# Two heads of a cross-attention in the two row halves of TensorE, scores in two matmuls each, values weighed every second slot

## The chip, the core and the metric

The kernel runs on one NeuronCore of a Trainium2 chip. TensorE (PE in the profile, its weight loads PEld) multiplies, VectorE (DVE) finds maxima, ScalarE (ACT) takes exponentials and copies, GpSimd (POOL) splits numbers, and the queue of SyncE (SP) issues DMAs. The metric is device microseconds of one execution: lower is better.

## The reference

The program computes two Perceiver layers: six blocks, each added to x (4 batches, 256 rows, 256 columns). Only the first block is touched by this change. It attends with 16 heads of 16 numbers from the 256 rows of x to a context of 4096 rows of 128 numbers:

```python
qh = (q @ Wq + bq).reshape(B, LQ, HEADS, D_K).transpose(0, 2, 1, 3)     # 4, 16, 256, 16
kh = (k @ Wk + bk).reshape(B, LKV, HEADS, D_K).transpose(0, 2, 1, 3)    # 4, 16, 4096, 16
vh = (v @ Wv + bv).reshape(B, LKV, HEADS, D_K).transpose(0, 2, 1, 3)
scores = jnp.einsum('bhqd,bhkd->bhqk', qh, kh) * scale
attn = jax.nn.softmax(scores, axis=-1)
out = jnp.einsum('bhqk,bhkd->bhqd', attn, vh)
x = x + out.transpose(0, 2, 1, 3).reshape(B, LQ, D_MODEL) @ Wo + bo
```

## The kernel before

`ContextAttention0` does this block. Queries and keys are float32, but their products are taken in bfloat16: each number is split into three bfloat16 parts, and of the nine products of parts the six largest are summed. They are summed by the contraction: `keysT` and `queriesT` hold six parts of 16 rows each under one another (`ROWS` = 96), and two more rows add the negative maximum of each query (its "shift", `AUG` = 98). Values and probabilities stay float32.

A *group* is two heads (`GH`) of one batch, 32 groups in all; four groups are a *unit*, eight a batch. A group has 16 *slots*; a slot is two tiles of 128 keys, 512 slots in all. TensorE's program is one loop over slots t, from -60 (the preparation) to 514. In a slot it does, in this order: scores of the first key tile of both heads (two matmuls of 256 columns, line 540), one matmul of 512 columns for the maxima of a group that lies `LEAD` = 19 slots ahead (line 524), scores of the second key tile, in every fourth slot the weighing of the last four slots (line 559), the second matmul for maxima, and then what the table `due` of `plan()` has for this slot:

- "fill keys" (line 587): 512 keys of a later unit, one float32 matmul, every 8 slots
- "make values" (line 626): two key tiles of the next batch's values, 16 times in a batch
- "turn ctx" (line 578): four transposes, 8 times in a batch
- "turn shift" (line 614) and "normalize" (line 645): once in a group

In three of the four batches this table is the same; the last has no next batch to prepare and has parts of the second block ("stream") instead. Each engine runs the same loop with its own part of each job, in its own program's order, and waits on semaphores.

PSUM has eight banks. Scores go through banks 0, 1 and 2 in turn (`HALVES`), the sums of the weighing through bank 3, and everything else, the maxima too, through 4, 5, 6 and 7 in turn (`misc`). A bank is written again once the engine that reads it has signalled: ACT after the exponential (line 783), DVE after the reduction of a matmul of maxima (line 685).

The weighing has 17 output partitions to a matmul, so four of them stand side by side in the 32-column strips of the array (`k.bank(SUMS)[32 * quad:...]`). All float32 matmuls appear in the trace as two records each.

Keys reach `keysT` through device memory: the parts are written by "write parts" and read back with three DMAs to a group, of 48, 32 and 16 rows to a head (`RUNS`). A group's maxima and scores wait until all of its DMAs have landed.

## Time and profile before

| | |
|---|---|
| median of 3 runs | 1429.02 us (1427.55 to 1429.71) |
| span of the profiled execution | 1429.1 us |
| TensorE's mean granted clock | 0.989 of full |
| first scores start, last weighing ends | 67.1 us, 968 us |
| PE busy | 1375.6 us, 96% |
| DVE, ACT, POOL busy | 74%, 65%, 20% |

The busy time of matmuls is modelled, and matmuls that follow each other overlap in it; what a matmul costs is read here as the distance from its start to the next start. The profiled execution shows its span alone, which lies within 0.1 us of the median.

### The profile page before, as it was taken

How to read it: one execution, taken by the hardware profiler on the slowest of the kernel's cores; microseconds unless marked ns; L12 is line 12 of the kernel's file. 1: busy time of each engine (PE TensorE's matmuls, PEld its weight loads, DVE VectorE, ACT ScalarE, POOL GpSimd, SP SyncE). 2: the span in 40 equal slices, each digit the busy share in tenths (PEclk: the TensorE clock that was granted, in tenths of full speed). 3: DMA queues.
4: the chain of work that ended last, by engine and by line, in shares of the span. 5: the costliest groups of instructions: out<-in, count | busy, mean ns of one | idle time of the engine just before them, and what ended most of it. 6: DMA issues, size and time to landing. Idle time of an engine off the chain costs nothing.

```text
span 1429.1 us, 28070 instructions
## 1 busy us (share of the span) xinstructions
PE 1375.6 (96%) x11138; PEld 846.7 (59%) x11138; DVE 1055.1 (74%) x2114; ACT 922.1 (65%) x1899; POOL 287.6 (20%) x321
## 2 busy tenths in 40 slices
PE   7799999999999999999999999999999999989998
PEld 5355555555555545555554556556557999856666
DVE  4787777787777778777778888835876778767757
ACT  5366777767777767777767666672796664448731
POOL 3354222222222222122213100000003100001210
PEclk9899999999999999999999999999999999999999
DMA  6966555346554545655454743002402320347000
GB/s 184 163 145 143 119 118 111 77 102 130 116 127 92 102 84 125 128 115 113 81 97 101 184 73 61 2 1 60 119 18 65 112 67 1 91 112 155 2 1 30
DMA packets 95587, 133.19 MB, mean 93 GB/s; under 512 B 8864, under 2 KB 70944, under 8 KB 89504
## 3 DMA queue, kind: packets, MB, share of 16 engines
q1 hardware_dynamic: 95456, 131.40, 42.3%
q8 instruction: 88, 1.44, 0.5%
q14 instruction: 43, 0.35, 0.1%
HBM read 94.15 MB, written 37.22 MB: 92 GB/s over the span
## 4 chain that ended last, share of the span: by engine, by line
PE 79%; ACT 8%; DVE 8%; DMA 2%; issue 2%; SPq 1%; POOL 0%; DVEq 0%; ACTq 0%
PE psum L559 16%; PE psum L540 13%; PE psum L524 13%; ACT probs L783 4%; PE psum L2132 4%; PE psum L587 3%; PE psum L2106 3%; DVE peaks L685 3%; PE psum L626 3%; PE psum L1226 2%; PE psum L2851 2%; PE psum L1623 1%; PE psum L275 1%; PE psum L2861 1%; PE psum L2814 1%
## 5 line engine op out<-in xcount | busy, mean ns | idle before, releaser
L685 DVE TENSOR_REDUCE peaks<-psum 128x1 f32<-128x512 f32 x1024 | 643.3, 684 | 197.0 <-PE psum L524 196.4
L783 ACT ACTIVATE probs<-psum 128x512 f32<-128x512 f32 x1024 | 529.0, 615 | 83.3 <-PE psum L540 79.4
L524 PE MATMUL psum<-keysT,queriesT 96*128 96x512 bf16 x1024 | 390.1, 384 | 13.2 <-DMA keysT<-key_parts 7.9
L540 PE MATMUL psum<-queriesT,keysT 98*128 98x256 bf16 x2048 | 392.4, 274 | 6.1 <-ACT queriesT L846 2.4
L540 PEld LDWEIGHTS psum<-queriesT,keysT 98*128 98x128 bf16 x2048 | 176.3, 99 | 191.7 <-ACT probs L783 72.1
L559 PE MATMUL psum<-probs,values 128*17 128x256 f32 x4096 | 245.9, 380 | 0.0
L559 PEld LDWEIGHTS psum<-probs,values 128*17 128x17 f32 x4096 | 107.2, 97 | 102.6 <-issue 27.1
L524 PEld LDWEIGHTS psum<-keysT,queriesT 96*128 96x128 bf16 x1024 | 98.6, 96 | 90.9 <-issue 56.1
L918 POOL CAST key_parts<-key_f 128x512 bf16<-128x512 f32 x57 | 34.8, 611 | 518.0 <-ACT key_f L816 511.0
L816 ACT ACTIVATE key_f<-psum,bk 128x512 f32<-128x512 f32 x59 | 40.5, 687 | 120.7 <-PE psum L587 120.6
L587 PE MATMUL psum<-ctxT,wk 128*128 128x512 f32 x128 | 69.5, 625 | 2.4 <-DVE probs L728 0.9
L924 POOL TENSOR_TENSOR key_parts<-key_r,key_parts 128x512 bf16<-128x512 f32 x57 | 66.0, 1158 | 4.5
L920 POOL TENSOR_TENSOR key_r<-key_f,key_parts 128x512 f32<-128x512 f32 x57 | 65.9, 1157 | 4.5
L2132 PEld LDWEIGHTS psum<-ctx_nat,ring 128*128 128x128 f32 x512 | 64.6, 191 | 3.6 <-ACT ring L2267 0.7
L2132 PE MATMUL psum<-ctx_nat,ring 128*128 128x129 f32 x512 | 65.9, 275 | 0.7 <-ACT ring L2267 0.6
L626 PE MATMUL psum<-wv,ctxT 128*128 128x256 f32 x256 | 65.4, 381 | 0.5 <-DVE probs L716 0.4
L1919 ACT ACTIVATE weights<-psum,peaks 128x256 f32<-128x256 f32 x128 | 58.7, 487 | 10.5 <-DVE peaks L1788 10.3
L2106 PE MATMUL psum<-early_weights,ctx_T 128*128 128x256 f32 x256 | 63.2, 380 | 0.0
L857 ACT ACTIVATE values<-psum 128x512 f32<-128x512 f32 x64 | 38.0, 599 | 29.3 <-PE psum L626 28.5
L2257 ACT ACTIVATE ring<-psum 128x512 f32<-128x512 f32 x64 | 37.7, 596 | 29.1 <-PE psum L2106 28.8
L626 PEld LDWEIGHTS psum<-wv,ctxT 128*128 128x128 f32 x256 | 47.9, 190 | 14.0 <-issue 5.5
L2267 ACT ACTIVATE ring<-ring 128x1024 f32<-128x1024 f32 (+1 forms) x36 | 34.6, 962 | 24.3 <-DVE ring L2177 24.1
(315 smaller groups left out, 1662.5 us busy)
## 6 DMA issues: line engine op xcount, KB each, us to landing
keysT<-key_parts SPq DMA_DIRECT2D x31, 768.0 KB, 7.7
key_parts<-key_parts SPq DMA_DIRECT2D x90, 256.0 KB
keysT<-key_parts SPq DMA_DIRECT2D x31, 512.0 KB, 10.1
ctx_nat<-in_ctx_dram SPq DMA_DIRECT2D x32, 256.0 KB, 3.0
keysT<-key_parts SPq DMA_DIRECT2D x31, 256.0 KB, 11.6
ctx_in<-in_ctx_dram SPq DMA_DIRECT2D x24, 256.0 KB, 5.9
ctx_turned<-ctxT SPq DMA_DIRECT2D x24, 256.0 KB, 4.4
ctx_T<-ctx_turned SPq DMA_DIRECT2D x12, 512.0 KB, 3.8
```

The lines of the kernel that those rows point to most:

```text
L524: e.matmul(ps, self.queriesT[0:ROWS, u % 2, g * GH + j, t * P:(t + 1) * P], self.keysT[0:ROWS, i % RING, j, c * BANK:(c + 1) * BANK], star ...
L540: made = e.matmul(ps[:, j * S:(j + 1) * S], self.keysT[0:AUG, i % RING, j, kt * P:(kt + 1) * P], self.queriesT[0:AUG, u % 2, g * GH + j, : ...
L559: made = e.matmul(k.bank(SUMS)[32 * quad:32 * quad + DH + 1, 0:S], self.values[b % 2][:, kt, g * GH + j, :], self.probs[:, (SLOTS * i + p) ...
L587: e.matmul(ps, self.wk[:, 0, m * P:(m + 1) * P], self.ctxT[:, c * BANK:(c + 1) * BANK], start=True, stop=True).then_inc(*self.key_made.up( ...
L626: made = e.matmul(ps[:, e2 * D:(e2 + 1) * D], self.ctxT[:, kt * P:(kt + 1) * P], self.wv[:, 0, :], start=True, stop=True)
L685: e.tensor_reduce(self.peaks[:, i % 2, pair, c:c + 1], k.ps(("max", n)), AX.X, ALU.max).then_inc(*self.peaked.up(n))
L783: e.activation(self.probs[:, t % RINGP, e2 * GH * S:(e2 + 1) * GH * S], k.ps(("scores", t, e2)), ACT.Exp).then_inc(*self.exped.up((t, e2)))
L920: e.tensor_tensor(self.key_r[:, :], k_f, part(0), ALU.subtract).then_inc(*w.up(self.split_pool, ("rest",) + key))
L924: e.tensor_tensor(part(2), self.key_r[:, :], part(1), ALU.subtract).then_inc(*w.up(self.split_pool, ("part2",) + key))
L1919: made = e.activation(self.weights[:, (2 * q + i) % self.NR, kt, :], k.ps(("scores3", q, i))[:, kt * S:(kt + 1) * S], ACT.Exp, bias=self.p ...
L2106: made = e.matmul(ps[:, i * S:(i + 1) * S], l.ctx_T[:, b % 2, kt * P:(kt + 1) * P], l.qcT[:, b * S:(b + 1) * S], start=True, stop=True)
L2132: made = e.matmul(k.ps(("weigh4", b, i))[:, 0:C + 1], self.at(n)[:, column:column + P], l.ctx_nat(b % 2)[:, kt, :], start=(kt == 0), stop= ...
```

## The change

A head's six products no longer stand in 98 rows. Each head has one half of the 128 rows: head 0 rows 0 to 63, head 1 rows 64 to 127. `keysT` and `queriesT` have two planes: MAIN holds four products (64 rows), REST the other two and the shift (34 rows). The scores of a key tile are now two matmuls to a head, MAIN and REST, summed in PSUM; the four matmuls of the two heads alternate between the halves. The maxima are taken over MAIN alone (four of the six products; the shift needs no more), and the matmuls of maxima of the two heads follow each other directly. A bank of scores now holds both key tiles of one head, and there are four such banks (0, 1, 2, 4); three are left for the rest (5, 6, 7). The weighing is done every second slot, in the odd ones, for two slots. Values, keys and transposes of the context are moved to even slots. Reads of keys are six DMAs of 32 rows instead of three; parts 0 and 1 of the queries are written twice.

```diff
 GH = 2
 PARTS = 3
 RUNS = ((0, 3), (3, 2), (5, 1))
-PAIRS = 6
-ROWS = PAIRS * DH
-AUG = ROWS + 2
+KEY_AT = (1, 2, 0)
+QUERY_AT = ((2, 3), (0, 1), (4,))
+HALF = P // 2
+MAIN, REST = 0, 1
+LOW = 2 * DH
+TALL = LOW + 2
 NG = H // GH
 GROUPS = B * NG
 SLOTS = LC // P // 2
@@ -308,7 +311,7 @@
 TOTAL = GROUPS * SLOTS
 FIRST = -60
 RINGP = 6
-HALVES, SUMS = 3, 3
+SCORES, SUMS, BLOCK = (0, 1, 2, 4), 3, 2
...
-        self.keysT = sb(scope, "keysT", [P, RING, GH, LC], BF16)
+        self.keysT = sb(scope, "keysT", [P, 2, RING, LC], BF16)
         self.values = [values, sb(scope, "values1", [P, LC // P, H, DH + 1])]
-        self.queriesT = sb(scope, "queriesT", [P, 2, P // DH, S], BF16)
+        self.queriesT = sb(scope, "queriesT", [P, 2, 2, UNIT_GROUPS, S], BF16)
...
-                slot = UNIT * u - 101 + 8 * c
+                slot = UNIT * u - 100 + 8 * c
...
-                at(SLOTS * NG * b - 97 + 6 * p, "make values", b, p)
+                at(SLOTS * NG * b - 96 + 8 * (p // 2) + 2 * (p % 2), "make values", b, p)
...
-            choice = (7, 0, 1, 2) if t < -1 else (4, 5, 6, 7)
+            choice = (7, 0, 1, 2) if t < -1 else (5, 6, 7)
...
-            e.matmul(ps, self.queriesT[0:ROWS, u % 2, g * GH + j, t * P:(t + 1) * P],
-                     self.keysT[0:ROWS, i % RING, j, c * BANK:(c + 1) * BANK],
-                     start=True, stop=True).then_inc(*self.max_made.up(n))
+            e.matmul(ps, self.queriesT[own, MAIN, u % 2, g, qt * P:(qt + 1) * P],
+                     self.keysT[own, MAIN, i % RING, c * BANK:(c + 1) * BANK],
+                     start=True, stop=True).then_inc(*self.max_made[j].up(n))
...
-            for e2 in range(2):
-                if 0 <= t < TOTAL:
-                    kt, n = 2 * p + e2, (2 * t + e2) % HALVES
-                    ps = banks.use(n, w, ("scores", t, e2), (self.exped, (t, e2)))
-                    for j in range(GH):
-                        made = e.matmul(ps[:, j * S:(j + 1) * S], self.keysT[0:AUG, i % RING, j, kt * P:(kt + 1) * P],
-                                        self.queriesT[0:AUG, u % 2, g * GH + j, :], start=True, stop=True)
-                    made.then_inc(*self.scored.up((t, e2)))
-                if maxima and not e2:
-                    find_max(maxima[0], t)
-            if t % 4 == 1 and 5 <= t <= TOTAL + 1:
-                i, p0 = divmod(t - 5, SLOTS)
+                ps = {}
+                for e2 in range(2):
+                    kt = 2 * p + e2
+                    for plane, rows in ((MAIN, HALF), (REST, TALL)):
+                        for j in range(GH):
+                            if j not in ps:
+                                ps[j] = banks.use(SCORES[(2 * t + j) % len(SCORES)], w, ("scores", t, j), (self.exped, (t, j)))
+                            own = slice(j * HALF, j * HALF + rows)
+                            made = e.matmul(ps[j][:, e2 * S:(e2 + 1) * S], self.keysT[own, plane, i % RING, kt * P:(kt + 1) * P],
+                                            self.queriesT[own, plane, u % 2, g, :], start=(plane == MAIN), stop=(plane == REST))
+                            if e2 and plane == REST:
+                                made.then_inc(*self.scored[j].up((t, j)))
+            for n in maxima:
+                find_max(n, t)
+            if t % BLOCK == 1 and BLOCK + 1 <= t <= TOTAL + 1:
+                i, p0 = divmod(t - BLOCK - 1, SLOTS)
                 b, g = divmod(i, NG)
                 w.wait_ge(self.exped, (t - 2, 1))
-                for p in range(p0, p0 + 4):
+                for p in range(p0, p0 + BLOCK):
                     w.wait_ge(self.v_kept, (b, p))
                 w.wait_ge(self.ones_set, b % 2)
                 if i:
                     w.wait_ge(self.outT_kept, i - 1)
                 w.wait_ge(self.cleared, 0)
-                for p in range(p0, p0 + 4):
+                for p in range(p0, p0 + BLOCK):
                     for e2 in range(2):
                         for j in range(GH):
-                            quad, kt = e2 * GH + j, 2 * p + e2
+                            quad, half, kt = e2 * GH + j, 2 * j + e2, 2 * p + e2
                             made = e.matmul(k.bank(SUMS)[32 * quad:32 * quad + DH + 1, 0:S],
                                             self.values[b % 2][:, kt, g * GH + j, :],
-                                            self.probs[:, (SLOTS * i + p) % RINGP, quad * S:(quad + 1) * S],
+                                            self.probs[:, (SLOTS * i + p) % RINGP, half * S:(half + 1) * S],
                                             start=(p == 0), stop=(p == SLOTS - 1))
-                made.then_inc(*self.weighed.up((t - 5) // 4))
-            for n in maxima[1:]:
-                find_max(n, t)
+                made.then_inc(*self.weighed.up((t - BLOCK - 1) // BLOCK))
...
-        return divmod(r, CH) if i else divmod(r, GH * QT)[::-1]
+        step, j = divmod(r, GH)
+        qt, c = divmod(step, CH) if i else divmod(step, QT)[::-1]
+        return i, j, qt, c
...
-                for e2 in range(2):
-                    w.wait_ge(self.scored, (t, e2))
-                    e.activation(self.probs[:, t % RINGP, e2 * GH * S:(e2 + 1) * GH * S], k.ps(("scores", t, e2)),
-                                 ACT.Exp).then_inc(*self.exped.up((t, e2)))
+                for j in range(GH):
+                    w.wait_ge(self.scored[j], (t, j))
+                    e.activation(self.probs[:, t % RINGP, 2 * j * S:(2 * j + 2) * S], k.ps(("scores", t, j)),
+                                 ACT.Exp).then_inc(*self.exped.up((t, j)))
...
-                    e.activation(self.queriesT[ROWS:AUG, u % 2, g * GH:(g + 1) * GH, :].rearrange("p h n -> p (h n)"),
-                                 k.ps(("shiftT", i)).bitcast(BF16)[ROWS:AUG, 0:GH * S], ACT.Copy).then_inc(
-                        *self.shiftT_kept.up(i))
+                    for j in range(GH):
+                        own = slice(j * HALF + LOW, j * HALF + TALL)
+                        e.activation(self.queriesT[own, REST, u % 2, g, :], k.ps(("shiftT", i)).bitcast(BF16)[own, 0:S],
+                                     ACT.Copy).then_inc(*self.shiftT_kept.up(i if j else ("first", i)))
...
-                        e.dma_start(self.q_dram[b, :, n, :, :, :].rearrange("h d m n -> h d (m n)"),
-                                    self.q_parts[:, n, :]).then_inc(*self.q_out.up(b))
+                        for copy in QUERY_AT[n]:
+                            e.dma_start(self.q_dram[b, :, copy, :, :, :].rearrange("h d m n -> h d (m n)"),
+                                        self.q_parts[:, n, :]).then_inc(*self.q_out.up(b))
...
-                    for block, run in RUNS:
-                        e.dma_start(self.queriesT[block * DH:(block + run) * DH, u % 2, :, :],
-                                    self.q_dram[b, :, 0:run, :, m, :].rearrange("h i d n -> (i d) h n")).then_inc(
-                            *self.rows_here[u % 2].up(u))
+                        for j in range(GH):
+                            w.wait_ge(self.scored[j], (UNIT * (u - 1) - 1, j))
+                    for plane, rows, parts in ((MAIN, HALF, slice(0, 4)), (REST, LOW, slice(3, 5))):
+                        for j in range(GH):
+                            e.dma_start(self.queriesT[j * HALF:j * HALF + rows, plane, u % 2, :, :],
...
-        for block, run in RUNS:
-            e.dma_start(self.keysT[block * DH:(block + run) * DH, i % RING, :, keys],
-                        self.key_dram[u, g * GH:(g + 1) * GH, PARTS - run:PARTS, :, keys].rearrange(
-                            "j i d n -> (i d) j n")).then_inc(*landed.up(key))
+        for j in range(GH):
+            for row, plane, first in ((0, MAIN, 1), (LOW, MAIN, 1), (0, REST, 0)):
+                e.dma_start(self.keysT[j * HALF + row:j * HALF + row + LOW, plane, i % RING, keys],
+                            self.key_dram[u, g * GH + j, first:first + 2, :, keys].rearrange("i d n -> (i d) n")).then_inc(
+                    *landed.up(key))
```

In the order of instructions on PE the change looks as follows in the middle of a unit (x counts matmuls as written). Names: `psum<-queriesT,keysT` are scores, `psum<-keysT,queriesT` maxima, `psum<-probs,values` the weighing, `ctxT,wk` the keys of a later unit. Before:

```order
L540 MATMUL psum<-queriesT,keysT 128x256 x2
L559 MATMUL psum<-probs,values 17x256 x16
L524 MATMUL psum<-keysT,queriesT 128x512
L587 MATMUL psum<-ctxT,wk 128x512
L540 MATMUL psum<-queriesT,keysT 128x256 x2
L524 MATMUL psum<-keysT,queriesT 128x512
L540 MATMUL psum<-queriesT,keysT 128x256 x2
L524 MATMUL psum<-keysT,queriesT 128x512
```

The same engine after the change, in the second half of a batch, from an odd slot over an empty even slot to one with keys and shift (lines are numbered anew: 546 scores, 527 maxima, 566 weighing, 592 keys, 620 shift):

```order
L566 MATMUL psum<-probs,values 17x256 x8
L546 MATMUL psum<-queriesT,keysT 128x256 x8
L527 MATMUL psum<-keysT,queriesT 128x512 x2
L546 MATMUL psum<-queriesT,keysT 128x256 x8
L527 MATMUL psum<-keysT,queriesT 128x512 x2
L566 MATMUL psum<-probs,values 17x256 x8
L546 MATMUL psum<-queriesT,keysT 128x256 x8
L527 MATMUL psum<-keysT,queriesT 128x512 x2
L592 MATMUL psum<-ctxT,wk 128x512
L620 MATMUL psum<-ident_b,shift_b 2x128 x4
```

What moved: the matmuls of maxima stand in pairs, the weighing comes in halves twice as often, and preparation never stands directly behind a weighing. Counted over the 512 slots, the array passes between full (128x128), column strips (128x32) and row halves (64x128) 882 times after and 316 times before.

The second place is the queue of SP in the preparation, from the first keys to the second write of keys. Before:

```order
L971 DMA key_parts<-key_parts 8x16x1024 x3
L996 DMA q_parts<-q_parts 8x16x512 x3
L1019 DMA keysT<-key_parts 48x2x1024
L1019 DMA keysT<-key_parts 32x2x1024
L1019 DMA keysT<-key_parts 16x2x1024
L1005 DMA queriesT<-q_parts 48x8x256
L1005 DMA queriesT<-q_parts 32x8x256
L1005 DMA queriesT<-q_parts 16x8x256
L971 DMA key_parts<-key_parts 8x16x1024 x3
```

After:

```order
L980 DMA key_parts<-key_parts 8x16x1024 x3
L1008 DMA q_parts<-q_parts 8x16x512 x5
L1034 DMA keysT<-key_parts 32x1024 x6
L1019 DMA queriesT<-q_parts 64x4x256 x2
L1019 DMA queriesT<-q_parts 32x4x256 x2
L980 DMA key_parts<-key_parts 8x16x1024 x3
```

Six more DMAs stand ahead of the second write of keys, in a queue that issues them one after another.

## Rows read from the trace of the kernel before

**Rows 1.** The page: span, and costliest groups (busy us, mean ns | idle before).

```profile
span 1429.1 us, 28070 instructions
...
L685 DVE TENSOR_REDUCE peaks<-psum 128x1 f32<-128x512 f32 x1024 | 643.3, 684 | 197.0 <-PE psum L524 196.4
...
L540 PEld LDWEIGHTS psum<-queriesT,keysT 98*128 98x128 bf16 x2048 | 176.3, 99 | 191.7 <-ACT probs L783 72.1
```

**Rows 2.** Stretches of 128 slots: length, then busy us of PE, PEld, DVE, ACT, POOL.

```profile
317.00:538.00 221.00, 219.39 (x1988) 118.50 (x1984) 167.52 (x306) 159.91 (x313) 56.60 (x64) 1.00 0.55 110
538.00:759.00 221.00, 219.40 (x1988) 118.53 (x1984) 167.51 (x306) 159.90 (x313) 56.61 (x64) 1.00 0.54 109
```

**Rows 3.** PE's timeline around a weighing (start us, modelled length, line).

```profile
502.39 0.38 PE L540 MATMUL psum<-queriesT,keysT 98*128 98x256 bf16 x2
502.61 0.38 PE L524 MATMUL psum<-keysT,queriesT 96*128 96x512 bf16 x1
502.83 0.38 PE L540 MATMUL psum<-queriesT,keysT 98*128 98x256 bf16 x2
...
505.33 0.39 PE L540 MATMUL psum<-queriesT,keysT 98*128 98x256 bf16 x2
505.65 1.92 PE L559 MATMUL psum<-probs,values 128*17 128x256 f32 x32
507.50 0.39 PE L524 MATMUL psum<-keysT,queriesT 96*128 96x512 bf16 x1
507.73 1.03 PE L626 MATMUL psum<-wv,ctxT 128*128 128x256 f32 x4
508.60 0.38 PE L540 MATMUL psum<-queriesT,keysT 98*128 98x256 bf16 x2
```

**Rows 4.** PE's timeline at a transpose of the context and at a shift.

```profile
340.68 0.60 PE L578 MATMUL psum<-const,ctx_in 128*128 128x128 f32 x4
341.12 0.38 PE L540 MATMUL psum<-queriesT,keysT 98*128 98x256 bf16 x2
...
541.40 0.38 PE L524 MATMUL psum<-keysT,queriesT 96*128 96x512 bf16 x1
541.71 0.38 PE L614 MATMUL psum<-ident_b,shift_b 128*2 128x128 bf16 x4
542.02 0.39 PE L540 MATMUL psum<-queriesT,keysT 98*128 98x256 bf16 x2
```

**Rows 5.** Waits: us in total, times, longest.

```profile
PEld psum L540 <- ACT probs L783: 72.1, 245, 0.8
```

**Rows 6.** PE's timeline in the third block: row strips (L1623), column strips (L1642).

```profile
1046.77 1.13 PE L1623 MATMUL psum<-qT,kT 32*128 32x256 f32 x8
1047.83 1.07 PE L1642 MATMUL psum<-weights,v_scaled 128*32 128x256 f32 x16
1048.83 1.16 PE L1623 MATMUL psum<-qT,kT 32*128 32x256 f32 x16
1049.92 0.42 PE L1642 MATMUL psum<-weights,v_scaled 128*32 128x256 f32 x4
```

**Rows 7.** Timelines of a matmul of maxima and of the reductions behind it.

```profile
46.75 1.38 DVE L685 TENSOR_REDUCE peaks<-psum 128x1 f32<-128x512 f32 x2
...
48.18 0.39 PE L524 MATMUL psum<-keysT,queriesT 96*128 96x512 bf16 x1 [0.31 <-DVE peaks L685]
...
500.86 0.39 PE L524 MATMUL psum<-keysT,queriesT 96*128 96x512 bf16 x1
...
501.29 0.69 DVE L685 TENSOR_REDUCE peaks<-psum 128x1 f32<-128x512 f32 x1 [1.34 <-PE psum L524]
502.59 4.28 DVE L685 TENSOR_REDUCE peaks<-psum 128x1 f32<-128x512 f32 x7 [0.61 <-PE psum L524]
```

**Rows 8.** The preparation: SP's timeline, and the chain that ended last.

```profile
18.04 2.71 SPq L996 DMA_DIRECT2D q_parts<-q_parts  x3
...
46.74 15.22 DMA keysT<-key_parts
```

More of the change, by code:

```diff
@@ L431, in plan @@
                 if c % 2:
-                    at(slot + 7, "write parts", u, c // 2)
+                    at(slot + 6, "write parts", u, c // 2)
         for u in range(B * KD):
@@ L978, in sync @@
                     n, first, last = CONST_COLS["ones"]
-                    for r in range(ROWS, AUG):
-                        e.dma_start(self.keysT[r:r + 1, :, :, :].rearrange("o r h n -> o (r h n)").bitcast(F32).rearrange(
-                            "o (p n) -> o p n", p=P), io["const"][:, first:last].unsqueeze(0)).then_inc(*self.ones_in.up(0))
+                    for r in (LOW, LOW + 1, HALF + LOW, HALF + LOW + 1):
+                        e.dma_start(self.keysT[r:r + 1, REST, :, :].rearrange("o r n -> o (r n)").bitcast(F32).rearrange(
+                            "o (p n) -> o p n", p=P), io["const"][:, first:(first + last) // 2].unsqueeze(0)).then_inc(
+                            *self.ones_in.up(0))
                 elif job == "load x":
```

39 lines of the change are left out of this document (21 added, 18 removed).

## The prediction

> **What bounds the kernel now.** I read the page first. One matmul of maxima is reduced in 684 ns on DVE, 1024 of them, and DVE has idle time in front of them that ends with TensorE; of TensorE's weight loads 72.1 us wait for the exponentials [rows 1, 5]. So ACT and DVE wait for PE most of the time, and PE for them some of it. The windows say how much: 128 slots, one batch, take 221.0 us, and PE is busy for 219.4 of them [rows 2]. A busy PE proves little, so I rebuilt the batch from start-to-start distances. Two score matmuls take 0.22 us and a matmul of maxima takes 0.22 [rows 3], so a slot is four such steps, 0.88. A weighing of 32 records takes 1.85 from 505.65 to 507.50. The two score matmuls ahead of it took 0.32 instead of 0.22, so going into column strips costs 0.10; a record of 256 float32 columns takes 0.87 / 4 = 0.217 alone, eight rounds of four side by side 1.73, so coming out costs 0.12 [rows 3]. Values take 0.87 [rows 3] and keys, two records of twice the columns, I count alike; a transpose of the context takes 0.44, a shift 0.31 + 0.09 [rows 4]; a gather of the heads I count like the shift, 0.40.
>
> A batch: 128 x 0.88 = 112.6, 32 weighings x 1.95 = 62.4, 32 keys and values x 0.87 = 27.8, 8 contexts x 0.44 = 3.5, 16 shifts and gathers x 0.40 = 6.4; together 212.7. Measured are 221.0, so PE itself is the bound, and 8.3 us of a batch are waits, most of them for the exponentials that hold the three score banks [rows 5].
>
> **The change part by part.** *Maxima.* Two matmuls of different row tiles can run side by side. The third block shows it: 8 records of 32 rows, two heads alternating, take 1.06 us (1046.77 to 1047.83), and 16 records of four heads take 1.09 [rows 6]. So a pair of maxima costs one matmul and a few ns, 0.23 instead of 0.44: 128 x -0.21 = -26.9 us a batch.
>
> *Scores.* Eight matmuls instead of four, in four rounds of two: 4 x 0.11 = 0.44 a slot, as before. Nothing is gained here; the same columns are streamed twice, by two heads at once. The bound from above is in the rivals.
>
> *Passages between tilings.* 0.10 in and 0.12 out [rows 3]; from column strips to row strips and back 1.00 - 0.87 = 0.13 and 1.06 - 0.87 = 0.19 with float32 weights that load longer [rows 6]. In a batch of the new order I count 224 passages against 79 (64 weighings and 44 even slots with a job, two each, and 8 between keys and shift). I take 0.105, near the bfloat16 rows: 145 x 0.105 = +15.2 us. The ends are 0.09 (+13) and 0.14 (+20). Nothing hides them, since they lie on PE. The Trainium skill (TensorEngine Tiling (Array Packing), section Tiling Modes) says that changing the tiling mode drains the array; the trace agrees, with 0.10 to 0.12 at each end of a weighing. By its speedup table alone, without that rule, the sum would keep the whole of the -26.9.
>
> *Three banks for maxima and jobs.* Both maxima of a slot are now issued together and need two of three banks. A reduction starts 0.43 after its matmul (500.86 to 501.29), the next 0.60 later ((4.28 - 0.68) / 6), each is 0.68 long, and PE starts 0.05 after its end (48.13 to 48.18) [rows 7]. So the first bank of a pair is free 1.16, the second 1.76 after the pair's start. How far away the next need is depends on the slot:
> - Even slot without a job (20 a batch, and some 90 in all): the next pair starts 0.23 + 0.44 = 0.67 later, and its second matmul needs the first bank: 1.16 - 0.68 = 0.48 of waiting; 9.6 us.
> - Context alone (4 a batch): the next pair is 0.67 + 0.44 + 0.22 = 1.33 away, and needs both banks: 0.43; with a gather as well (4) the gather itself waits some 0.4. Gather alone (4): 0.5. Together 5.3 us.
> - Keys and values (32): 0.67 + 0.87 + 0.22 = 1.76 away, just enough: 0.02, 0.6 us.
> Together +15.5 us a batch. From below it is 0, if PE would have stood still there anyway; the odd slots leave it no such excuse, as DVE has 2.4 us of work in the 2.4 us of PE of an empty even and an odd slot.
>
> *Waits that go.* Four score banks hold two whole slots, and ACT has 160 us of work in 221 [rows 2]; a weighing lasts 0.87 instead of 1.73. I expect almost all of the 8.3 to go and leave 1: -7.3. What is late next is the second matmul of maxima in odd slots.
>
> *Keys, values, contexts moved to even slots:* the same work, 0. They are what keeps the even slots from being empty. *Two small copies of the shift instead of one* lie on ACT, a slot and a half ahead of their use: 0.
>
> *Preparation.* SP issues the writes of queries at 2.71 / 3 = 0.90 each [rows 8]; two more are 1.8, five more reads in that stretch some 0.45 each, 2; SP stood waiting for landings for part of it. What ends the preparation is a read of keys that takes 15.2 us [rows 8] and moves the same bytes as before. I take +3, between 0 and +6.
>
> **The sum.** A batch: -26.9 + 15.2 + 15.5 - 7.3 = -3.5. The last batch has no keys and values, more empty slots and as few passages; I count it alike. 4 x -3.5 = -14, for gaps between my rows and a real batch (keys with a shift, three normalizations of x) +3, preparation +3: -8. The span 1429.1 becomes 1421; span and median lie within 0.1 us, so the median too.
>
> **The rivals.** *Slower by dear passages.* If each passage costs 0.14 as between strips in the third block, the 566 more that the order shows cost 79 instead of 59, and 1421 becomes 1441. The place is the exit of each weighing and each job in an even slot; the sum changes sign at 0.12. For it: the exit at 507.50 already shows 0.12, and the first two weight loads of a row pair come unprepared. Against it: the extra in the third block is with float32 weights.
>
> *Much slower: the weights of the two halves are loaded one after another.* A slot has eight loads of scores, 99 ns each [rows 1], 0.79 instead of 0.44: +0.35 x 512 = +179 less the waits that vanish in it, about 1580. Against it: 16 loads to 1.09 us in the third block [rows 6], 68 ns each and of float32. This is also the case in which the change does not do what it says. The Trainium skill (TensorE: Matmul & The Clock Gate, section LDWEIGHTS) says that a load's time goes by its columns and not by its rows, so 34 rows load no faster than 128; the page's 128 / 1.2, an estimate of 107 ns, would give 0.85 a slot and some 1600.
>
> *Faster: full array to row halves is cheap.* If only the column strips of the weighing cost a passage, 312 passages x 0.105 = -33, about 1388. For it: no bfloat16 row shows this passage. Against it: a shift, bfloat16 in column strips, shows 0.09 on entering [rows 4].
>
> *Faster by less waiting.* If the 0.48 of the even slots were mostly there before as other waits, up to -25: 1396.
>
> **How the numbers follow.** Forecast (PE bound, passages near 0.105, bank waits as worked out, 1400 to 1436): 0.58. Dear passages or more waits, 1433 to 1450: 0.24. Serial weights: 0.06. Cheap passages or fewer waits, 1385 to 1400: 0.12. A measurement of this kernel can tell 0.2%, 2.9 us. Of the forecast two thirds lie under 1426, a sixth within 0.2%; with the other cases faster 0.53, same 0.12, slower 0.35. The range leaves out the serial weights and the ends of the other cases: 1390 to 1447.
>
> **What would show it.** Matmuls of maxima in pairs under 10 ns apart, and then 0.22 to the next start: the gain. Two score matmuls starting together and 0.11 to the next two. In odd slots behind an empty even one, the second matmul of maxima starts about 0.48 after the first, with DVE's reduction as releaser. PE's steps around each weighing and each job 0.09 to 0.12 longer than the columns. Loads of scores waiting for exponentials nearly gone. A batch of 217 to 218 us instead of 221.0, and first scores near 70 us. I am wrong if the two halves don't overlap, if DVE (167.5 us of work in a batch) makes PE wait in most slots and not in the few that I counted, or if keys land late, which would show as long waits of the first maxima of a group for DMAs.

## The result, and the profile after

Measured side by side, the changed kernel takes 1445.26 us (median of 4 runs, 1441.35 to 1447.82) and the kernel before 1429.37 (1427.55 to 1430.82): a ratio of 1.0091, 95% interval 1.0065 to 1.0117 (the two medians alone give 1.011). It became 0.9% slower where 0.6% faster was forecast. The profiled execution is the fastest of the four. In the runs on record the time is about 1.8 us longer than the span of the same execution, and so the span before, 1429.1 us, fits the slowest of its four runs, 1430.82, and not the median. The profiled span after is 1439.6 us, 10.5 more than before; the accounts below are made against that span.

The page of the changed kernel, its costliest groups (busy us, mean ns | idle before, and what ended it):

```profile
L693 DVE TENSOR_REDUCE peaks<-psum 128x1 f32<-128x512 f32 x1024 | 650.2, 685 | 192.4 <-PE psum L527 191.3
...
L546 PEld LDWEIGHTS psum<-queriesT,keysT 64*128 64x128 bf16 (+1 forms) x4096 | 168.5, 95 | 176.0 <-ACT probs L791 121.3
...
L527 PEld LDWEIGHTS psum<-keysT,queriesT 64*128 64x128 bf16 x1024 | 68.6, 94 | 99.7 <-DVE peaks L693 83.6
```

The last row is the new one: the weight loads of the maxima (line 527) now wait 83.6 us for reductions. The row of scores names 121.3 us of waits for exponentials, more than before [rows 5]. That alone says little: a loader that has nothing to do while the array is still busy is idle too. What counts is the distance from start to start on PE.

The windows, one for each batch, from its first scores to those of the next, for the last batch to those of its last slot (length, then busy us of PE, PEld, DVE, ACT, POOL). After:

```profile
66.70:298.90 232.20, 226.09 (x2517) 111.95 (x2517) 175.41 (x322) 172.61 (x330) 74.95 (x86) 0.99 0.47 119
298.90:520.80 221.90, 217.31 (x2500) 105.89 (x2496) 170.17 (x306) 168.20 (x322) 56.53 (x65) 1.00 0.45 110
520.80:742.70 221.90, 217.31 (x2500) 105.92 (x2496) 170.17 (x306) 168.09 (x322) 56.54 (x65) 1.00 0.45 109
742.70:975.40 232.70, 219.96 (x2518) 116.88 (x2516) 174.06 (x353) 154.24 (x299) 25.53 (x28) 1.00 0.29 72
```

And before, the first and the last batch (the middle ones are in [rows 2]):

```profile
67.10:296.70 229.60, 225.24 (x1988) 124.32 (x1987) 173.22 (x322) 163.82 (x321) 75.36 (x86) 1.00 0.55 117
738.70:962.80 224.10, 217.65 (x2021) 127.22 (x2022) 172.55 (x354) 150.82 (x292) 25.29 (x28) 1.00 0.37 74
```

So the batches changed by +2.6, +0.9, +0.9 and +8.6 us, where the forecast had -3.5 for each. The preparation is 0.4 us shorter (66.7 against 67.1) and what follows the last weighing 1.5 shorter.

PE's timeline of the changed kernel in a middle batch (start us, modelled length, line) has nearly every kind of slot that holds a job:

```profile
430.34 0.62 PE L546 MATMUL psum<-queriesT,keysT 64*128 64x256 bf16 x8
430.80 0.38 PE L527 MATMUL psum<-keysT,queriesT 64*128 64x512 bf16 x2
431.11 1.06 PE L566 MATMUL psum<-probs,values 128*17 128x256 f32 x16
432.10 0.62 PE L546 MATMUL psum<-queriesT,keysT 64*128 64x256 bf16 x8
...
432.86 0.66 PE L583 MATMUL psum<-const,ctx_in 128*128 128x128 f32 x4
433.45 0.62 PE L546 MATMUL psum<-queriesT,keysT 64*128 64x256 bf16 x8
433.91 0.79 PE L527 MATMUL psum<-keysT,queriesT 64*128 64x512 bf16 x2
434.63 1.06 PE L566 MATMUL psum<-probs,values 128*17 128x256 f32 x16
...
436.07 0.38 PE L527 MATMUL psum<-keysT,queriesT 64*128 64x512 bf16 x2
436.38 1.13 PE L592 MATMUL psum<-ctxT,wk 128*128 128x512 f32 x2
437.44 0.28 PE L620 MATMUL psum<-ident_b,shift_b 128*2 128x128 bf16 x4
437.65 0.62 PE L546 MATMUL psum<-queriesT,keysT 64*128 64x256 bf16 x8
438.11 0.57 PE L527 MATMUL psum<-keysT,queriesT 64*128 64x512 bf16 x2
438.60 0.63 PE L566 MATMUL psum<-probs,values 128*17 128x256 f32 x8
```

Eight scores take 0.45 or 0.46 us to the next start (430.34 to 430.80), as forecast. The pair of maxima at 430.80 takes 0.31 with the passage into column strips, so 0.22 and 0.09: the halves do run side by side. The weighing takes 0.99, 0.87 and 0.12 for the passage out. At 433.91 the pair has a length of 0.79 and 0.72 to the next start instead of 0.31: there the second matmul waited for a bank, 0.41 us, behind a transpose of the context. At 438.11 it waited again, 0.49 instead of 0.31, behind a slot with keys and a shift, for which the forecast had 0.02.

An odd slot behind an empty even one, from the same kernel's PE timeline in the second batch:

```profile
312.78 0.60 PE L546 MATMUL psum<-queriesT,keysT 64*128 64x256 bf16 x8
313.22 0.89 PE L527 MATMUL psum<-keysT,queriesT 64*128 64x512 bf16 x2
314.04 1.06 PE L566 MATMUL psum<-probs,values 128*17 128x256 f32 x16
```

The pair takes 0.82 to the next start instead of 0.31: its second matmul starts 0.50 behind the first, where the forecast had 0.48.

### The profile page after: what moved, and what is told of

It reads as the page before. It is cut to its first block, busy times and chain, and to the rows that moved or that the text cites. A ratio compares the mean times of both kernels' runs of the same rounds, so it can differ in the third digit from the quotient of the medians.

```text
span 1439.6 us, 32414 instructions
## 1 busy us (share of the span) xinstructions
PE 1372.3 (95%) x13186; PEld 794.0 (55%) x13186; DVE 1064.8 (74%) x2114; ACT 950.5 (66%) x1931; POOL 287.2 (20%) x321
## 4 chain that ended last, share of the span: by engine, by line
PE 76%; DVE 17%; ACT 3%; issue 2%; DMA 1%; SPq 1%; POOL 0%; DVEq 0%; POOLq 0%; ACTq 0%
PE psum L566 16%; PE psum L546 14%; DVE peaks L693 10%; PE psum L527 9%; PE psum L592 5%; PE psum L632 4%; PE psum L2147 4%; PE psum L2121 3%; PE psum L1241 2%; PE psum L2866 2%; PE psum L2876 1%; PE psum L275 1%; PE psum L1638 1%; ACT weights L1934 1%; PE psum L2829 1%
## 5 line engine op out<-in xcount | busy, mean ns | idle before, releaser
L693 DVE TENSOR_REDUCE peaks<-psum 128x1 f32<-128x512 f32 x1024 | 650.2, 685 | 192.4 <-PE psum L527 191.3
L791 ACT ACTIVATE probs<-psum 128x512 f32<-128x512 f32 x1024 | 546.2, 599 | 200.5 <-PE psum L546 195.3
L546 PE MATMUL psum<-queriesT,keysT 64*128 64x256 bf16 (+1 forms) x4096 | 316.3, 272 | 0.0
L527 PE MATMUL psum<-keysT,queriesT 64*128 64x512 bf16 x1024 | 254.2, 382 | 26.0 <-DVE peaks L693 11.5
L566 PE MATMUL psum<-probs,values 128*17 128x256 f32 x4096 | 270.8, 382 | 0.0
L546 PEld LDWEIGHTS psum<-queriesT,keysT 64*128 64x128 bf16 (+1 forms) x4096 | 168.5, 95 | 176.0 <-ACT probs L791 121.3
L566 PEld LDWEIGHTS psum<-probs,values 128*17 128x17 f32 x4096 | 94.1, 96 | 115.0 <-issue 64.6
L527 PEld LDWEIGHTS psum<-keysT,queriesT 64*128 64x128 bf16 x1024 | 68.6, 94 | 99.7 <-DVE peaks L693 83.6
L592 PE MATMUL psum<-ctxT,wk 128*128 128x512 f32 x128 | 75.3, 671 | 5.4 <-DVE peaks L693 3.1
L632 PE MATMUL psum<-wv,ctxT 128*128 128x256 f32 x256 | 70.8, 402 | 0.5 <-DVE probs L724 0.4
L1934 ACT ACTIVATE weights<-psum,peaks 128x256 f32<-128x256 f32 x128 | 58.6, 487 | 10.5 <-DVE peaks L1803 10.3
L632 PEld LDWEIGHTS psum<-wv,ctxT 128*128 128x128 f32 x256 | 43.9, 189 | 22.8 <-DVE peaks L693 11.5
L2282 ACT ACTIVATE ring<-ring 128x1024 f32<-128x1024 f32 (+1 forms) x36 | 34.6, 961 | 24.3 <-DVE ring L2192 24.1
```

The source lines that it names most:

```text
L527: e.matmul(ps, self.queriesT[own, MAIN, u % 2, g, qt * P:(qt + 1) * P], self.keysT[own, MAIN, i % RING, c * BANK:(c + 1) * BANK], start=Tr ...
L546: made = e.matmul(ps[j][:, e2 * S:(e2 + 1) * S], self.keysT[own, plane, i % RING, kt * P:(kt + 1) * P], self.queriesT[own, plane, u % 2, g ...
L566: made = e.matmul(k.bank(SUMS)[32 * quad:32 * quad + DH + 1, 0:S], self.values[b % 2][:, kt, g * GH + j, :], self.probs[:, (SLOTS * i + p) ...
L592: e.matmul(ps, self.wk[:, 0, m * P:(m + 1) * P], self.ctxT[:, c * BANK:(c + 1) * BANK], start=True, stop=True).then_inc(*self.key_made.up( ...
L632: made = e.matmul(ps[:, e2 * D:(e2 + 1) * D], self.ctxT[:, kt * P:(kt + 1) * P], self.wv[:, 0, :], start=True, stop=True)
L693: e.tensor_reduce(self.peaks[:, i % 2, j * QT + qt, c:c + 1], k.ps(("max", n)), AX.X, ALU.max).then_inc(*self.peaked.up(n))
```

## The experiments

They are read by one table: the time from the first scores of an even slot to those of the next even slot, by the job that the even slot holds (medians of all such pairs of slots in the second batch, us). The forecast for them comes from the terms on record: no job 2 x 0.67 + 0.87 + 0.21 + 0.48 = 2.90; values or keys 2 x 0.67 + 1.08 + 0.87 + 0.21 + 0.02 = 3.52; keys and shift, with 0.40 and one more passage, 4.03. The last column is the whole second batch, from first scores to first scores.

| | no job | values | keys | keys, shift | context | gather | context, gather | batch |
|---|---|---|---|---|---|---|---|---|
| forecast | 2.90 | 3.52 | 3.52 | 4.03 | 3.50 | 3.53 | 3.87 | 217.5 |
| changed kernel | 2.93 | 3.59 | 3.58 | 4.15 | 3.52 | 3.52 | 3.94 | 221.9 |
| 1: maxima first in even slots | 2.48 | 3.58 | 3.58 | 4.09 | 3.11 | 3.09 | 3.80 | 209.8 |
| 2: banks 3 and 4 | 3.12 | 3.59 | 3.58 | 3.79 | 3.12 | 3.09 | 3.52 | 219.4 |
| 3: maxima apart | 2.70 | 3.59 | 3.58 | 4.15 | 3.30 | 3.30 | 3.80 | 215.1 |
| 7: half reductions | 2.66 | 3.59 | 3.58 | 3.98 | 3.11 | 3.09 | 3.67 | 210.5 |
| 8: jobs behind weighing | 2.48 | 3.54 | 3.69 | 4.05 | 3.07 | 3.04 | 3.60 | 207.5 |

### 1. Maxima ahead of the scores in even slots

```diff
+            if t % 2 == 0:
+                for n in maxima:
+                    find_max(n, t)
             (scores)
-            for n in maxima:
-                find_max(n, t)
+            if t % 2:
+                for n in maxima:
+                    find_max(n, t)
```

> The changed kernel, but in even slots the pair of matmuls for maxima stands ahead of the scores instead of behind them; in odd slots it stays behind the scores. No matmul is added, and the passages between tilings stay 882. Theory A (in empty even slots and slots with a short job the second matmul of maxima waits for a bank, about 0.45 us each time): two slots without a job fall from 2.93 us to about 2.47, two slots with a context transpose or a gather from 3.52 to about 3.05, those with keys or values stay at 3.6; a batch falls from 221.9 us to about 208, the kernel to about 1390 us. Rival B (the passages alone explain the loss, the bank waits only fill time in which TensorE would stand for exponentials or for DVE's throughput anyway): a batch stays within 3 us of 221.9 and the kernel within 12 us of 1445.

Measured: 1397.75 us (1395.62 to 1400.09), ratio to before 0.9766, interval 0.9723 to 0.9809. The window of a middle batch:

```profile
499.40:709.20 209.80, 209.24 (x2498) 105.62 (x2496) 170.37 (x305) 165.53 (x321) 56.56 (x65) 1.00 0.48 115
```

It is 12.1 us shorter than the changed kernel's, with the same instructions: the same pairs, the same passages, only the pair of the even slot 0.45 us earlier and so further from the next. Pairs of slots with no job, a context or a gather alone fall by 0.41 to 0.45; those with values or keys stay. This shows the three banks' wait: 12.1 us of a middle batch go with the order of two lines, where the sum had 15.5 for all of it. The wait does not go whole; a context with a gather, and keys with a shift, still wait (3.80, 4.09).

### 2. Three banks for scores, four for the rest

```diff
-SCORES, SUMS, BLOCK = (0, 1, 2, 4), 3, 2
+SCORES, SUMS, BLOCK = (0, 1, 2), 3, 2
...
-            choice = (7, 0, 1, 2) if t < -1 else (5, 6, 7)
+            choice = (7, 0, 1, 2) if t < -1 else (4, 5, 6, 7)
```

> The changed kernel with the banks shared out as before the change: three for scores (0, 1, 2), four for maxima and jobs (4 to 7). Theory A: the waits of the second matmul of maxima go (two slots without a job lose 0.48 us of them), but the scores of an odd slot behind an empty even one now need the bank whose exponential ends some 0.5 us later, so that wait takes its place; the kernel stays within 12 us of 1445, with weight loads of scores waiting for exponentials in place of those of maxima waiting for DVE. Rival B (four score banks buy nothing, only the loss of the fourth other bank costs): a batch falls by some 14 us and the kernel to about 1390 us.

Measured: 1433.73 us (1431.74 to 1438.48), ratio 1.0028, interval 1.0004 to 1.0052. A middle batch takes 219.4. PE's timeline in one:

```profile
518.43 0.38 PE L527 MATMUL psum<-keysT,queriesT 64*128 64x512 bf16 x2
518.64 0.27 PE L546 MATMUL psum<-queriesT,keysT 64*128 64x256 bf16 x1
519.27 0.61 PE L546 MATMUL psum<-queriesT,keysT 64*128 64x256 bf16 x7 [0.36 <-ACT probs L791]
519.62 0.48 PE L527 MATMUL psum<-keysT,queriesT 64*128 64x512 bf16 x2
520.04 1.06 PE L566 MATMUL psum<-probs,values 128*17 128x256 f32 x16
```

The fourth bank of the rest takes the wait of the maxima away, and the scores of the next slot now wait for ACT: 3.12 with no job, more than 2.93. With a context or gather it is 0.4 less, and with keys and shift 3.79 instead of 4.15. That last one is the news: such a slot takes two more banks of the ring of three, and its wait is 0.36, not 0.02. In the changed kernel's timeline all eight such pairs of the second batch wait 0.18 at the maxima behind the job, and four of them 0.35 more ahead of it.

### 3. The two maxima of a slot apart

The first behind the scores of the first key tile, the second behind those of the second, so that they are never issued together:

```diff
+                    if maxima and not e2:
+                        find_max(maxima[0], t)
-            for n in maxima:
+            for n in (maxima[1:] if 0 <= t < TOTAL else maxima):
                 find_max(n, t)
```

> The changed kernel with the two matmuls for maxima of a slot taken apart: the first behind the scores of the first key tile, the second behind those of the second, so that they can't run side by side. Theory A (a pair saves one matmul of 0.22 us, part of which is given back as a wait for a bank): two slots with values or keys grow from 3.59 to about 4.0 us, two slots without a job stay near 2.9; a batch grows by 12 to 17 us and the kernel to about 1500 us. Rival (running side by side saves nothing that lasts, because DVE takes 0.60 us for each anyway): the kernel stays within 10 us of 1445.

Measured: 1418.16 us (1417.53 to 1423.53), ratio 0.9918, interval 0.9890 to 0.9945, some 80 us under what I expected. PE's timeline says why:

```profile
434.74 0.39 PE L546 MATMUL psum<-queriesT,keysT 64*128 64x256 bf16 x4
434.98 0.38 PE L527 MATMUL psum<-keysT,queriesT 64*128 64x512 bf16 x1
434.98 0.48 PE L546 MATMUL psum<-queriesT,keysT 64*128 64x256 bf16 x3
435.20 0.38 PE L527 MATMUL psum<-keysT,queriesT 64*128 64x512 bf16 x1
435.30 0.27 PE L546 MATMUL psum<-queriesT,keysT 34*128 34x256 bf16 x1
435.51 1.13 PE L634 MATMUL psum<-wv,ctxT 128*128 128x256 f32 x4
```

The matmul of maxima of head 0 starts at 434.98, and scores of head 1 start in the same hundredth beside it. From the first scores to the job it is 0.77, as with pairs (435.62 to 436.38, 0.76). So what the forecast called a pair is not needed: each half works through its own matmuls, whatever the other does, as long as both have the same number of columns to take in a stretch. The Trainium skill (TensorEngine Tiling (Array Packing), Tiling Modes) says that tiles operate independently of each other; the trace agrees, with 512 columns in one half beside 256 at a time in the other. The second maximum now comes 0.22 after the first and not with it, and slots without a job fall from 2.93 to 2.70.

### 4. Weighing every second slot, alone

The kernel before, with this one part of the change:

```diff
-            if t % 4 == 1 and 5 <= t <= TOTAL + 1:
-                i, p0 = divmod(t - 5, SLOTS)
+            if t % 2 == 1 and 3 <= t <= TOTAL + 1:
+                i, p0 = divmod(t - 3, SLOTS)
...
-                for p in range(p0, p0 + 4):
+                for p in range(p0, p0 + 2):
...
```

> The kernel before the change with one part of the change alone: the weighing is done every second slot for two slots, in the odd ones; everything else is as before. Theory A (each further weighing costs two passages between tilings, 0.10 + 0.12 us): 128 more weighings cost 28 us, less some of the 8 us a batch that TensorE waits for exponentials behind long weighings; the kernel comes to 1440 to 1457 us. Rival (a shorter weighing keeps ACT and DVE fed and pays for its passages): at or below 1429 us.

Measured: 1426.80 us (1421.70 to 1431.61), ratio 0.9972, interval 0.9950 to 0.9995. A middle batch takes 220.8 against 221.0, although it has 32 more weighings, that is 64 passages or 6.7 us. The waits of this kernel in total (us, times, longest), where before had 72.1 [rows 5]:

```profile
PEld psum L540 <- ACT probs L783: 25.3, 86, 0.8
```

The passages are paid by the waits for exponentials that a weighing of 1.73 us had caused. So the -7.3 of the forecast was real, and comes with this part of the change and its passages: the part is worth about nothing. That holds while the maxima come one by one; experiment 2 shows that in pairs, with three banks for scores, waits for exponentials come back.

### 5. Weighing every fourth slot, in the changed kernel

Its edit is `BLOCK = 4`.

> The changed kernel with one part undone: the weighing is done every fourth slot for four slots, as before the change. 128 weighings and 256 passages between tilings go. Theory A: the passages save 7 us a batch, but now every other odd slot has no weighing either, so that pairs of maxima follow each other at 0.67 us and the second waits for its bank in more slots; four slots without a job take 6.1 us instead of 5.86, with two jobs 7.4 instead of 7.2; a batch grows from 221.9 to about 229, the kernel to about 1475 us. Rival (passages decide): a batch falls to 215, the kernel to about 1417 us.

Measured: 1486.94 us (1482.94 to 1491.10), ratio 1.0390, interval 1.0358 to 1.0423. A middle batch is 9.7 us longer (231.6) with 64 passages fewer. PE's timeline behind a weighing:

```profile
546.24 0.83 PE L546 MATMUL psum<-queriesT,keysT 64*128 64x256 bf16 x8
546.83 0.39 PE L527 MATMUL psum<-keysT,queriesT 64*128 64x512 bf16 x1
547.43 0.39 PE L527 MATMUL psum<-keysT,queriesT 64*128 64x512 bf16 x1 [0.21 <-DVE peaks L693]
548.02 0.63 PE L653 MATMUL psum<-const,outT 128*128 128x34 f32 x4 [0.21 <-DVE peaks L693]
```

With no weighing between them, one slot after the other waits for the ring, and in the end the gather too.

### 6. Jobs in their old, odd slots, in the changed kernel

```diff
-                slot = UNIT * u - 100 + 8 * c
+                slot = UNIT * u - 101 + 8 * c
...
-                at(SLOTS * NG * b - 96 + 8 * (p // 2) + 2 * (p % 2), "make values", b, p)
+                at(SLOTS * NG * b - 97 + 6 * p, "make values", b, p)
```

The writes of key parts are kept in the slots in which they were.

> The changed kernel with another part undone: keys, values and context stand in the slots in which they stood before the change, the odd ones, behind a weighing. Theory A: 4.6 us of passages go in a batch, but nearly all even slots are now empty or short, and each of these costs 0.45 to 0.5 us of waiting for a bank: 31 us of such waits in a batch instead of 15.5; a batch grows from 221.9 to about 232, the kernel to about 1485 us. Rival (passages decide): a batch of 217, the kernel at about 1427 us.

Measured: 1480.25 us (1478.21 to 1481.13), ratio 1.0329, interval 1.0306 to 1.0353; a middle batch 234.2. More even slots stand empty, and each costs its wait: in the second batch the loads of the maxima wait 34.1 us for reductions, in the changed kernel 13.7. Without the move of the jobs the change would have cost some 35 us more.

### 7. Half of each reduction

```diff
-                e.tensor_reduce(..., k.ps(("max", n)), AX.X, ALU.max)
+                e.tensor_reduce(..., k.ps(("max", n))[:, 0:BANK // 2], AX.X, ALU.max)
```

> The changed kernel, but each reduction on DVE reads only the first 256 of the 512 columns of its bank, so that half of the maxima are left out (the shift is then not the true maximum); TensorE's work is unchanged. Theory A: a reduction takes about 0.33 us instead of 0.60, the two banks are free 0.9 and 1.2 us after the pair's start; two slots without a job fall from 2.93 to about 2.66, with context or gather from 3.52 to about 3.1, those with keys or values stay at 3.59; a batch falls by 10 to 12 us to about 211. The last batch, 232.6 us, falls by more, 13 us or more, if its excess comes from DVE, which has jobs of the second block there; if it comes from ScalarE or from data that arrives late, it falls by no more than the others. The kernel comes to about 1398 us. Rival B (bank waits are not the cause): within 5 us of 1445.

Measured: 1387.14 us (1385.44 to 1387.86), ratio 0.9682, interval 0.9660 to 0.9704. The middle batches fall by 11.4 us to 210.5, the last by 17.0, from 232.6 to 215.6. So in the middle a faster DVE is worth what earlier maxima are worth (experiment 1), and in the last batch it is worth half as much again. Half of the maxima are left out here, so this is a test of the cause and no kernel to use.

The waits for reductions in the last batch show the same. Before (us, times, longest):

```profile
PEld psum L524 <- DVE peaks L685: 8.3, 21, 1.1
...
PE psum L524 <- DVE peaks L685: 2.3, 3, 0.8
```

After:

```profile
PEld psum L527 <- DVE peaks L693: 24.9, 44, 1.8
...
PE psum L527 <- DVE peaks L693: 7.0, 15, 1.4
```

With half reductions:

```profile
PEld psum L527 <- DVE peaks L693: 11.7, 31, 1.5
...
PE psum L527 <- DVE peaks L693: 3.5, 4, 1.1
```

The loads' waits (PEld) and the array's own (PE) overlap in part and are not to be added, but both are three times those before, and with half reductions both fall by half. What makes DVE late there stands in its timeline, here with PE's, of the changed kernel:

```profile
847.40 0.69 DVE L1400 TENSOR_TENSOR x<-psum,x 128x512 f32<-128x512 f32 x1 [1.60 <-PE psum L1241]
847.75 0.38 PE L527 MATMUL psum<-keysT,queriesT 64*128 64x512 bf16 x2
...
848.12 0.43 DVE L1323 BATCH_NORM_STATS2 small<-x 128x6 f32<-128x256 f32 x1
848.41 0.38 PE L527 MATMUL psum<-keysT,queriesT 64*128 64x512 bf16 x1
...
849.40 1.88 DVE L693 TENSOR_REDUCE peaks<-psum 128x1 f32<-128x512 f32 x3
850.15 0.39 PE L527 MATMUL psum<-keysT,queriesT 64*128 64x512 bf16 x1 [1.36 <-DVE peaks L693]
```

An addition to x and the statistics of the second block's normalization hold DVE from 847.40 to 849.40. The pair of 847.75 is reduced 1.65 us after its start, not 0.43, and the second matmul of the next pair starts 1.74 behind its first, not 0.50. Three slots of the last batch wait like this one (at 848.4, 915.8 and 943.0).

### 8. All jobs in odd slots, behind the weighing

On top of experiment 1, with the shift ahead of the keys. Values and gathers move by one slot as well; their lines are left out here.

```diff
-                slot = UNIT * u - 100 + 8 * c
+                slot = UNIT * u - 101 + 8 * c
...
-            at(SLOTS * i - 2, "turn shift", i)
+            at(SLOTS * i - 3 if i else -2, "turn shift", i)
```

> Maxima placed as in x1_maxima_first, and all preparation (keys, values, context, shift, gather) moved from the even slots to the odd ones, where it stands directly behind the weighing; the shift ahead of the keys. A job then costs one passage between tilings more instead of two, a shift none. Theory A (passages at 0.10 to 0.12 us each are what is left to save, and with the maxima ahead of the scores the empty even slots no longer cost a wait): against x1_maxima_first a batch falls by some 44 x 0.105 = 4.6 us and by the bank wait of keys with a shift (0.3 us, 8 times), from 209.8 to about 203, the kernel from 1398 to about 1373 us. Rival (even distribution of the work over odd and even slots is what keeps ACT and DVE fed; with long odd slots they run dry): at or above 1398 us.

Measured: 1393.52 us (1392.10 to 1396.04), ratio 0.9734, interval 0.9710 to 0.9758. A middle batch takes 207.5, 2.3 less than in experiment 1 where 7 was expected. Each job now has one passage fewer, which should have given 0.1. Values and keys with a shift gained 0.04, a context with a gather 0.20, but keys alone cost 0.11 more. Against values in the same kernel these take 0.15 more, and in the trace the extra stands at the maxima ahead of the weighing and not at the job; what holds them there, the runs don't tell.

### 9. and 10. The four maxima of two slots one by one

Experiment 8, and then experiment 1, with the pairs split: in even slots one ahead of the scores and one between the key tiles, in odd slots one between them and one behind.

```diff
...
+                    if maxima and not e2:
+                        find_max(maxima[(t + 1) % 2], t)
...
```

> Edit: the kernel with maxima ahead of the scores in even slots and all jobs behind the weighing of odd slots (median 1393.5), now with the four maxima of two slots one by one: in an even slot the first ahead of the scores and the second between the two key tiles, in an odd slot the first between the key tiles and the second behind them, ahead of the weighing. A (the row halves work as two streams, and DVE then gets its matmuls some 0.65 us apart): a matmul of maxima still costs half of 0.22 in its own half, the 18 us of waits of TensorE for the reductions in 200 us mostly go, a batch takes 205 instead of 207.5 in the middle and the last one 215 instead of 223: about 1378. B (a single maximum between scores leaves the other half idle for part of its 0.22): four times up to 0.11 in two slots, up to 28 us a batch, 1400 to 1500. C (the waits only move to the exponentials): 1390 to 1396.

> Edit: the same spreading of the maxima, on the kernel that has maxima ahead of the scores in even slots and the jobs in even slots as the change put them (median 1397.8). A: the distances between two maxima are then nearly even also where a job stands (job behind the even slot, weighing behind the odd one), so a batch falls from 209.8 to 206 or 207 and the last one from 223 to 216: about 1380. B: no gain in the middle batches, since the waits left there are not DVE's: 1392 to 1398. C (single maxima cost up to 0.11 each): over 1400.

Measured: 1390.57 us (1385.99 to 1391.99), ratio 0.9720, interval 0.9686 to 0.9753, and 1394.03 (1391.15 to 1395.42), ratio 0.9747, interval 0.9717 to 0.9778. Each split gains 0.7 to 0.9 us in a middle batch (207.5 to 206.6, 209.8 to 209.1): the single maxima cost nothing, as the two streams would have it, but there was little left to gain. The last batch takes 221.4 and 221.1, 1.3 and 1.9 less, and most of its waits for reductions stay. The first of the two has the lowest median of the kernels here that leave nothing out, 2.8% under before, but its interval overlaps that of experiment 8.

## Why the prediction was wrong

**What held.** PE bound the kernel and still does. The pair of maxima costs one matmul (0.22 against 0.44), and scores cost the same. A passage takes 0.09 to 0.12 around a weighing, and an empty pair of slots 2.93 for 2.90. The waits for exponentials went: in the two middle batches of the changed kernel eight scores take 0.44 to 0.46 to the next start in every slot, and experiment 4 shows which part of the change did it. Loads in the two halves do overlap, eight of them in that same 0.46. The three banks were sized well where the forecast had a wait: summed over the second batch, slots with nothing, a context or a gather wait 14.9 us, and the terms for them were 9.6 + 5.3 = 14.9. That it fits to the tenth is luck, since an empty slot waited 0.50 for 0.48 and a gather 0.43 for 0.5.

**The steps that failed.** Of the 18.6 us by which the span missed, 4.4 lie in each of the four batches, 7.7 more in the last and 1.7 more in the first; other terms missed by 8.4 the other way.

**In every batch: +0.9 for -3.5, the price of jobs.** Added up by pairs of slots, as in the table above (20 with no job, 24 with values or keys, 8 with keys and shift, 4 of each of the rest), my terms make 218.3 and not 217.5: the 0.40 of a shift or gather holds a passage that is counted there again, and the 1 us of waits that I left is not in the pairs. The measured medians make 221.7. The difference of 3.4 is 1.5 for values and keys, 1.0 for keys with a shift (8 times 0.12), 0.5 for the empty ones and 0.3 for the rest. Two steps were wrong. "Keys and values (32) ... just enough: 0.02" leaves out that a shift takes a bank of the ring too: 0.36 (experiment 2), partly made up for by a shift that took 0.21 to the next start and not 0.40. And "I take 0.105" for each passage is too little for a job: values take 1.06 to the next start where the forecast had 0.87 + 0.105. The trace says where it goes. A view of this line's instructions from 429.0 to 430.5 (ns min, median, max):

```profile
L632 PE MATMUL psum<-wv,ctxT x4: 379/379/483, 429.3 to 430.0; 128*128 128x256 f32 x4
```

One of the four records takes 0.10 longer, and it is the first: it starts at 429.28 and the second at 429.60, while the others follow each other at 0.215. The passage out takes 0.10. The loads of this job after (L632) and before (L626), where it stood between bfloat16 matmuls of the full array and took 0.87 [rows 3]:

```profile
429.27 0.30 PEld L632 LDWEIGHTS psum<-wv,ctxT 128*128 128x128 f32 x2 [0.32 <-DVE peaks L693]
```

```profile
507.51 0.63 PEld L626 LDWEIGHTS psum<-wv,ctxT 128*128 128x128 f32 x3
```

Before, the first weights were loaded 0.22 ahead of their matmul, which starts at 507.73; after, the load starts with its matmul. The releaser that the view names is not the cause: with four banks in the ring (experiment 2) the same job takes the same 1.06. That weights can't be loaded ahead of a passage fits this and is not shown by a test of its own.

**In the last batch: "The last batch has no keys and values, more empty slots and as few passages; I count it alike."** It grew by 8.6 us where -3.5 was counted, 7.7 more than a middle one. Two things lie behind it. First, I had looked at what PE no longer does there and not at what DVE does instead. The bound with three banks rests on reductions starting 0.43 after their matmul; in the last batch DVE has the second block's small jobs in between. In experiment 7 the last batch falls by 5.6 us more than a middle one, so about that much is DVE against its ring of banks. Experiment 2 shows that the ring alone is not the way out: with four banks for it the last batch still takes 232.0, and its loads of scores wait 46.7 us for exponentials instead of 18.5. Second, maxima run 19 slots ahead (`LEAD`), so the last 19 slots have none and the pair saves nothing there. The matmuls of maxima in the second and in the last batch (length, then busy us and count of PE and PEld):

```profile
298.90:520.80 221.90, 61.09 (x256) 16.90 (x256) 1.00 0.45 110
742.70:975.40 232.70, 57.34 (x218) 15.12 (x218) 1.00 0.29 72
```

That is an estimated 19 x 0.21 = 4.0 us less gain, against which stand 131 further passages instead of 145, 1.5 us. 5.6 + 4.0 - 1.5 = 8.1, against 7.7; no experiment tests the second part alone.

**The first batch: +2.6 for -3.5.** 4.4 of these 6.1 us are those of every batch. In its first 3.0 us (66.7 to 69.7) TensorE had a granted clock of 0.50, that is the lower level of 1.2 GHz, and before only in the first 1.2 us (67.1 to 68.3, 0.51); by an estimate, half of the 1.8 us between them, this is 0.9 us. For the other 0.8 the runs show no cause.

**The other way:** +3 for the preparation (measured -0.4), +3 for gaps, a tail 1.5 shorter than assumed, and 0.5 less from the last slot's scores to the last weighing. 4 x 4.4 + 7.7 + 1.7 - 3.4 - 3 - 1.5 - 0.5 = 18.6. The median missed by 24.3: 3.9 more since the profiled execution is the fastest of its runs, and 1.8 since "span and median lie within 0.1 us" set a span equal to a time, which is about 1.8 longer.

**The rivals and the chances.** "Dear passages or more waits, 1433 to 1450" had 0.24, and the time came there, by some of both. "Dear passages" as it was told, 0.14 each, fell: the exit of a weighing takes 0.12 and its entry 0.09; only float32 jobs of the full array are dearer. Serial weights fell too. "Less waiting", 1396, did not happen, but experiment 1 shows that it was to be had, by the order of the maxima. With it a batch falls 11.2 us under the one before, so the row halves do bring what the sum promised of them; what took it back is that maxima in pairs meet a ring of three banks.

## What to carry to other kernels

When a change halves the time between two requests for a buffer, work out the wait for each pattern of neighbours, all takers of the ring included, and do it again for each stretch in which the engine that frees the buffers has other jobs. If a fast pair must wait for a slow reader, first spread the requests in time before giving more buffers: here the order of two lines was worth some 47 us, a bank moved from one ring to the other some 10. And a stretch that "has less to do" on the bounding engine may be the one where another engine's lateness shows, and the one in which the part that gains has nothing left to do.

## What was not expected of the hardware

- The two row halves are two independent streams: a matmul of 512 columns in one half beside matmuls of 256 in the other, both starting at 434.98 (experiment 3). In experiments 3, 9 and 10 only the sum of the columns of each half mattered, not which matmuls stood together.
- A float32 job of values or keys, full array between row halves, costs 0.29 beyond its columns: 0.09 on the way in, 0.10 in its first record and 0.10 on the way out. A weighing in column strips has 0.21.
- Twice as many weighings of half the length cost nothing (ratio 0.9972, experiment 4): the waits for exponentials fell from 72.1 to 25.3 us.
